# Edge weights in a PSUM bank of their own, and one bank for the state-space products

## The reference, cut to what matters

```python
proj = (x @ gat_w.T).reshape(n, NH, FOUT)                    # 4 heads of 64
e = leaky_relu(s_src[src] + s_tgt[tgt], 0.2)
exp_e = exp(e - max(e))
denom = segment_sum(exp_e, tgt)
agg = segment_sum(proj[src] * (exp_e / denom[tgt])[:, :, None], tgt)
...
xc, z = split(xs @ in_proj_w.T)          # xs = x[perm]
xc = silu(conv4(xc) + conv_b)
dbc = xc @ x_proj_w.T                    # 16 for dt, 16 for B, 16 for C
dt = softplus(dbc[:, :16] @ dt_proj_w.T + dt_proj_b)
h = exp(dt * A) * h + (dt * xc) * B      # scan over the nodes, 16 states per channel
y = (h @ C + xc * D_param) * silu(z)
out = y @ out_proj_w.T
```

## The kernel before, in words

| slot of TensorE | bank 0 | bank 1 |
|---|---|---|
| 2 | transpose of the input, `mb_x` (L1090) | output projection, `mb_y` (L1079) |
| 4 | turning of the output, `mb_o` (L1129) | input projection, first half (L1079) |
| 6 | input projection, second half (L1079) | |
| 9 | | projection to B, C, dt (L1106) |
| 11 | dt projection (L1113) | |

## Time and profile before

### The profile page before, as it was taken

One profiled execution on the slowest core, in us unless ns is written; L12 is line 12 of the kernel. 1 busy time (PEld: TensorE's weight loads), 2 busy tenths in 40 slices (PEclk: granted clock), 3 DMA queues, 4 the chain that ended last, 5 costly groups with the idle time before them and its releaser, 6 DMA issues. The chain is left out here.

```text
span 4467.2 us, 66228 instructions
## 1 busy us (share of the span) xinstructions
PE 3254.4 (73%) x18333; PEld 2554.5 (57%) x18334; DVE 3342.3 (75%) x6618; ACT 1430.2 (32%) x2818; POOL 2574.3 (58%) x2215
## 2 busy tenths in 40 slices
PE   5344220488878878888888888888888488848998
PEld 4333210366666666666666666666666345527887
DVE  5677793699988988899888898989888568831111
ACT  2000000244433344333443333443333256622222
POOL 2000004477777777777777777777777246643443
PEclk8555555599999999999999999999999699979999
DMA  3000201233333333333333333333335523326665
GB/s 109 20 0 0 96 1 59 75 97 97 97 96 98 99 96 96 95 95 98 97 96 96 96 97 98 96 97 96 93 99 91 109 58 98 85 84 151 143 143 110
DMA packets 217329, 397.02 MB, mean 89 GB/s; under 512 B 49239, under 2 KB 137544, under 8 KB 216776
## 3 DMA queue, kind: packets, MB, share of 16 engines
q0 software_dynamic: 119472, 287.74, 26.3%
q1 hardware_dynamic: 97560, 105.54, 7.7%
HBM read 330.21 MB, written 62.91 MB: 88 GB/s over the span
## 5 line engine op out<-in xcount | busy, mean ns | idle before, releaser
L664 POOL DMA_INDIRECT el_g<-table,el_ix x1792 | 2026.4, 1131 | 623.2 <-issue 455.3
L1050 PE MATMUL fl_ps<-el_g,el_oh 128*128 128x260 f32 x3584 | 935.3, 406 | 303.3 <-DVE ACC L773 300.3
L1050 PEld LDWEIGHTS fl_ps<-el_g,el_oh 128*128 128x128 f32 x3584 | 695.0, 200 | 662.1 <-issue 534.2
L929 ACT COPY el_oht<-fl_pt 128x512 f32<-128x512 f32 x452 | 262.7, 581 | 1217.3 <-PE fl_pt L1027 1217.3
L793 DVE TENSOR_TENSOR_SCAN mb_h<-mb_dA,mb_h,mb_dB 128x224 f32<-128x224 f32 x896 | 572.9, 669 | 85.3 <-issue 62.4
L763 DVE TENSOR_TENSOR el_g<-el_g 128x1024 f32<-128x1024 f32 x448 | 544.3, 1215 | 0.0
L1039 PEld LDWEIGHTS fl_px<-tile_score,el_oht 128*128 128x128 f32 x3608 | 484.1, 198 | 72.4 <-issue 53.5
L1039 PE MATMUL fl_px<-tile_score,el_oht 128*128 x3608 | 456.0, 256 | 28.3 <-issue 27.3
L1073 PE MATMUL fl_py<-mb_hc,ident 128*128 128x448 f32 x896 | 436.6, 570 | 0.1
L938 ACT ACTIVATE mb_dA<-mb_dt,mb_a 128x224 f32<-128x224 f32 x898 | 382.9, 476 | 106.4 <-DVE mb_dt L854 104.6
L1027 PE MATMUL fl_pt<-ident,el_oh 128*128 128x128 f32 x1808 | 302.4, 292 | 151.2 <-DVE el_oh L730 150.4
(11 more groups left out here) (290 smaller groups left out, 5161.4 us busy)
## 6 DMA issues: line engine op xcount, KB each, us to landing
el_g<-table,el_ix POOLq DMA_INDIRECT x1792, 2.8
ex_w<-in_moe_W SPq DMA_DIRECT2D x56, 512.0 KB
ex_x<-routed_x SPq DMA_DIRECT2D x56, 257.0 KB, 2.7
mb_x<-sorted_x SPq DMA_DIRECT2D x30, 224.0 KB, 2.8
table<-px_tr POOLq DMA_DIRECT2D x49, 130.0 KB, 2.4
px_x<-in_x SPq DMA_DIRECT2D x49, 128.0 KB, 2.8
xn<-XN SPq DMA_DIRECT2D x1, 6272.0 KB
sorted_y<-mb_or SPq DMA_DIRECT2D x28, 224.0 KB, 2.5
```

Of the source, the lines that this page charges most:

```text
L664: pool.indirect_dma_start(out=G[b // GU][:, b % GU * NJ + j, :], out_offset=None, in_=dram["table"], in_offset=bass.IndirectOffsetOnAxis(a ...
L1050: mm = nc.tensor.matmul(pS[:], OH[:, n % (2 * GU), j, :], G[n // GU % 2][:, n % GU * NJ + j, :], start=j == 0, stop=j == NJ - 1)
```

## The change

The weights get a PSUM bank of their own, `fl_pw`. ScalarE still writes the exponentials into `el_g` right after the logits, and writes them a second time into `fl_pw` at the end of its slot, after `give_out`, `prepare` and the decay; only the second write signals "weight". Since `fl_pw` holds one group of four slots, the second write waits until VectorE has scaled the last slot of the group before. The scaling reads the weights from `fl_pw` instead of from `el_g`.

To free that bank, all state-space products share one bank, `fl_pm`, so they follow each other: input transposed in TensorE's slot 0 (copied by ScalarE in slot 1), output projection in 2 (copied in 3), input projections in 4 and 6 (copied in 5 and 7), output turned in 8 (copied by ScalarE in slot 8 too), B, C and dt in 9 (10), dt projection in 11 (11). SyncE stores the output chunk after slot 10 instead of 6.

```diff
-        pY, pM = ps("fl_py", [P, KD, TC]), [ps(f"fl_pm{b}", [P, 512]) for b in range(2)]
+        pY, pM, pW = ps("fl_py", [P, KD, TC]), ps("fl_pm", [P, 512]), ps("fl_pw", [P, 512])
+        weight = pW[:, 0:GU * NJ * NH].rearrange("p (c h) -> p c h", h=NH)
...
-                nc.vector.tensor_tensor(rows, rows, G[g][:, at, D:].unsqueeze(3).to_broadcast([P, NJ, NH, FO]),
+                nc.vector.tensor_tensor(rows, rows, weight[:, at, :].unsqueeze(3).to_broadcast([P, NJ, NH, FO]),
...
             def prepare(c, b, at):          # ScalarE
-                if at == 3:
+                if at == 1:
                     act.wait_ge(s["xT"], c + 1)
-                    nc.scalar.copy(XT[:], wide(pM[0])).then_inc(s["xT_sb"], 1)
+                    nc.scalar.copy(XT[:], wide(pM)).then_inc(s["xT_sb"], 1)
...
             def give_out(c, at):            # ScalarE
-                elif at == 5:
+                elif at == 8:
                     act.wait_ge(s["oT"], c + 1)
...
-                    nc.scalar.copy(OR[:], pM[0][0:RB, :].rearrange("p (r d) -> p r d", r=TS)).then_inc(s["oT_sb"], 1)
+                    nc.scalar.copy(OR[:], pM[0:RB, :].rearrange("p (r d) -> p r d", r=TS)).then_inc(s["oT_sb"], 1)
...
             def slot(S):                    # ScalarE
-                    nc.scalar.activation(G[n // GU % 2][:, :, D:], DM[:], ACT.Exp).then_inc(s["weight"], 1)
+                    nc.scalar.activation(G[n // GU % 2][:, :, D:], DM[:], ACT.Exp)
                 if not early(c, 1):
                     give_out(c - 1, at)
                 prepare(c + 1, 1 - b, at)
                 decay(S + 1)
+                if n % GU == 0:
+                    if not early(S.number, 1):
+                        act.wait_ge(s["scaled"], S.number)
+                    nc.scalar.activation(weight, DM[:], ACT.Exp).then_inc(s["weight"], 1)
...
             def prepare(c, b, at):          # TensorE
-                if at == 2:
+                if at == 0:
                     pe.wait_ge(s["x"], (c + 1) * 16)
...
                 elif at == 6:
+                    pe.wait_ge(s["in_sb"], c + 1)
+                    project(pM, WI, XT, KD).then_inc(s["z_in"], 1)
+                elif at == 9:
+                    pe.wait_ge(s["z_sb"], c + 1)
                     if not early(c, 2):
                         pe.wait_ge(s["oT_sb"], c - 1)
...
             def give_out(c, at):            # TensorE
                 if at == 2:
                     pe.wait_ge(s["gated"], c + 1)
-                    pe.wait_ge(s["dt_row"], c + 2)
-                    pe.wait_ge(s["bx_rest"], c + 2)
-                    project(pM[1], WO, Y, 0).then_inc(s["o"], 1)
-                elif at == 4:
+                    pe.wait_ge(s["xT_sb"], c + 3)
+                    project(pM, WO, Y, 0).then_inc(s["o"], 1)
+                elif at == 8:
                     pe.wait_ge(s["o_sb"], c + 1)
-                    pe.wait_ge(s["xT_sb"], c + 3)
+                    pe.wait_ge(s["z_sb"], c + 3)
+                    turn_out()
```

More of the change, by code:

```diff
@@ L697, in slot @@
                     load(c + 2)
-                if at == 6 and not early(c, 1):
+                if at == 10 and not early(c, 1):
                     store(c - 1)
@@ L948, in prepare @@
                     act.wait_ge(s["in"], c + 1)
-                    nc.scalar.copy(XR[:, :, CONV - 1:], wide(pM[1])).then_inc(s["in_sb"], 1)
+                    nc.scalar.copy(XR[:, :, CONV - 1:], wide(pM)).then_inc(s["in_sb"], 1)
                 elif at == 7:
                     act.wait_ge(s["z_in"], c + 1)
-                    nc.scalar.activation(SZ[:, b], wide(pM[0]), ACT.Silu).then_inc(s["z_sb"], 1)
+                    nc.scalar.activation(SZ[:, b], wide(pM), ACT.Silu).then_inc(s["z_sb"], 1)
                 elif at == 8:
@@ L960, in prepare @@
                     act.wait_ge(s["bx"], c + 1)
-                    nc.scalar.copy(PARTS[0:2 * NS, b, :], pM[1][0:2 * NS, 0:TC]).then_inc(s["bx_hi"], 1)
+                    nc.scalar.copy(PARTS[0:2 * NS, b, :], pM[0:2 * NS, 0:TC]).then_inc(s["bx_hi"], 1)
                     act.wait_ge(s["bx_rest"], c + 1)
-                    nc.scalar.copy(DTR[2 * NS:, :], pM[1][2 * NS:BX, 0:TC]).then_inc(s["dt_row"], 1)
+                    nc.scalar.copy(DTR[2 * NS:, :], pM[2 * NS:BX, 0:TC]).then_inc(s["dt_row"], 1)
                     act.wait_ge(s["bx_mid"], c + 1)
@@ L984, in give_out @@
                     act.wait_ge(s["o"], c + 1)
-                    nc.scalar.copy(O[:], wide(pM[1])).then_inc(s["o_sb"], 1)
-                elif at == 5:
+                    nc.scalar.copy(O[:], wide(pM)).then_inc(s["o_sb"], 1)
+                elif at == 8:
                     act.wait_ge(s["oT"], c + 1)
@@ L1012, in _ @@
             give_out(NC - 1, 3)
[L1013 removed]
+            give_out(NC - 1, 8)
         @block.tensor
@@ L1110, in prepare, with turn_out @@
                     pe.wait_ge(s["dt_row"], c + 1)
-                    pe.wait_ge(s["z_sb"], c + 1)
+                    pe.wait_ge(s["bx_rest"], c + 1)
                     for m in range(KD):
-                        mm = nc.tensor.matmul(wide(pM[0])[:, m, :], WD[2 * NS:, m * P:(m + 1) * P], DTR[2 * NS:, :],
+                        mm = nc.tensor.matmul(wide(pM)[:, m, :], WD[2 * NS:, m * P:(m + 1) * P], DTR[2 * NS:, :],
                                               start=True, stop=True, skip_group_check=True)
                     mm.then_inc(s["dt_in"], 1)
+            def turn_out():
+                for r in range(TS):
+                    for k in range(KD):
+                        mm = nc.tensor.transpose(pM[0:RB, r * D + k * P:r * D + (k + 1) * P],
+                                                 O[:, k, r * RB:(r + 1) * RB], w["ident"][:])
+                mm.then_inc(s["oT"], 1)
             def give_out(c, at):
@@ L1119, in give_out @@
                     pe.wait_ge(s["gated"], c + 1)
-                    pe.wait_ge(s["dt_row"], c + 2)
-                    pe.wait_ge(s["bx_rest"], c + 2)
-                    project(pM[1], WO, Y, 0).then_inc(s["o"], 1)
-                elif at == 4:
+                    pe.wait_ge(s["xT_sb"], c + 3)
+                    project(pM, WO, Y, 0).then_inc(s["o"], 1)
+                elif at == 8:
                     pe.wait_ge(s["o_sb"], c + 1)
-                    pe.wait_ge(s["xT_sb"], c + 3)
-                    for r in range(TS):
-                        for k in range(KD):
-                            mm = nc.tensor.transpose(pM[0][0:RB, r * D + k * P:r * D + (k + 1) * P],
-                                                     O[:, k, r * RB:(r + 1) * RB], w["ident"][:])
-                    mm.then_inc(s["oT"], 1)
+                    pe.wait_ge(s["z_sb"], c + 3)
+                    turn_out()
             def slot(S):
@@ L1158, in _ @@
             pe.wait_ge(s["gated"], NC)
-            project(pM[1], WO, Y, 0).then_inc(s["o"], 1)
+            pe.wait_ge(s["v"], (NC + 1) * KD)
+            project(pM, WO, Y, 0).then_inc(s["o"], 1)
             pe.wait_ge(s["o_sb"], NC)
-            for r in range(TS):
-                for k in range(KD):
-                    mm = nc.tensor.transpose(pM[0][0:RB, r * D + k * P:r * D + (k + 1) * P],
-                                             O[:, k, r * RB:(r + 1) * RB], w["ident"][:])
-            mm.then_inc(s["oT"], 1)
+            turn_out()
 def nodes(nc, sem, w, a, dram):
```

14 lines of the change are left out of this document (5 added, 9 removed).

## The result

The changed kernel takes 4550.51 us (median of 4, 4549.45 to 4553.80), the kernel before 4478.07 beside it (4472.79 to 4479.94): a ratio of 1.0167, interval 1.0151 to 1.0183. The forecast was 4555.0. The profiled execution took 4550.16 and its span 4548.4, 81.2 us more than before, at the same mean granted clock of 0.868.

The account below looks back on a forecast made before the run. VectorE was busiest (75%), but ScalarE was taken as the bound in slots 8 and 9. 75.6 + 22 - 15 - 3, less 2 for gather waits, gave +78 on 4477: 4555 us, range 4530 to 4580.

Parts of the forecast that it names:

- The wait that the change puts in slot 8: ScalarE's copy in slot 8 waits for TensorE's turning; VectorE's wait before slot 9's scan grows 1.70 to 4.50: +75.6 us.
- Nothing swallowed: Later waits, the only candidate being slot 12's put down to gathers, absorb none of the 75.6 us.
- The rival that counted on 31 us: Partly swallowed: gather waits in slot 12 absorb 31 us, clock falls no more often; +27, 4504 us; chance 12%.
- rows 8 and 9: Slot 12's waits for gather or scores plus decay, in two chunks: 2.12 and 2.13 us together.
- The clock: TensorE's longer idle gap in slot 9 lowers its clock every chunk; 15 of 26 get new 1.5 us `mb_parts` waits: +22.
- The give-back in slot 4: Input transposes leave TensorE's slot 2 for slot 0, so slot 4's scores come 0.54 us earlier: 27 times, -15 us.
- The scaling: VectorE's scaling from PSUM gains at most 15 ns, 448 times; about half swallowed: -3 us, range -7 to +7.
- The rival of a much faster scaling: At L763 the PSUM operand shortens each scaling by 0.25 us, giving 4443 us; chance 4%.
- the estimate in the prediction: By the skill page's access overheads (about 60 ns SBUF, 125 ns PSUM), the scaling would cost 29 us more.
- At nothing: Costs counted as zero: second exponential behind the decay (32 us if uncovered), other moved copies, SyncE, everything outside the loop.
- GpSimd: By the skill's contention rule its gathers get shorter, but it is not awaited except in 43.9 us of waits.
- the dearer rival: TensorE comes back slow (+50 instead of +22) and PSUM reads cost 7: +118, 4595 us; chance 9%.

Follow-up runs that it names:

- The stall alone: Kernel before, two banks and weights in SBUF kept, only the output's turning and its copy moved to slot 8 (store to 10): 4807.59 us, 1.0302.
- second group: Follow-up kernels run on one chip where the kernel before took 4665.44 us; the changed kernel took 4874.85 us there, 1.0456.
- the stall undone: Changed kernel with ScalarE copying the turned output in slot 9 instead of 8: 4789.17 us (1.0244), repeated at 4788.60 us (1.0232).
- the shared bank alone: Changed kernel without the second exponential (weights read from SBUF) and with the turned output copied in slot 9: 4468.06 us, 0.9957.
- third group: Follow-up kernels run on a chip like that of the first comparison; the kernel before took 4490.51 us there.
- first group: Follow-up kernels run on one chip where the kernel before took 4669.68 us; the changed kernel itself was not among them.
- the decay first: Kernel before with ScalarE making the next slot's decay ahead of give_out and prepare: 4407.75 us, 0.9820.

## Why the prediction was right

The forecast was +78 us and the measured difference is +72.4 of the medians, +81.2 of the two profiled spans. The largest term and its mechanism are right; that the total fits so well is partly luck. The costs were forecast at 97.6 us (75.6 and 22) and come to 110 in VectorE's intervals over 26 chunks; the gains were forecast at 20 (15, 3 and 2) and come to 34, of which 22 lie in places for which the sum has no term (slots 0, 6 and 8). The two misses nearly cancel. Point by point:

- **The wait that the change puts in slot 8.** Right in place, cause and nearly in size: 4.42 instead of 1.70 in front of the scan of slot 9, where 4.50 was forecast. That is 27 x 2.72 = 73 us for the term of 75.6; in the last chunk alone it is 6.81. The stall alone brings a slowdown in the old kernel, undoing it gives 86 us in the second group, and without it and without the PSUM weights the kernel is at 0.9957. So the stall is shown to be the cause, and the shared bank is shown not to be. The stall was not undone by itself on a chip like that of the first comparison.
- **Nothing swallowed.** Right. Slot 12 kept its wait (2.11 per chunk before, 2.25 after). Of the 43.9 us "for gathers" the waits in slot 12, some 32 us, had been a label: they went away without a gain, and the wait for the decay grew by 23.4. The five in slot 8 were real but small, apart from one of 6.28 at the loop's end, which stays at 5.54. The rival that counted on 31 us fell on rows 8 and 9, as argued.
- **The clock.** The mechanism was right, the size too small: `mb_parts` is waited for in 27 places, not 11, with 1.69 each instead of 1.5, so +29 for the term of +22. The granted clock of 0.58 behind the gap and the vanishing of these waits when the gap was filled both show that it is the clock. Why filling it gained no time on its chip stays open.
- **The give-back in slot 4.** This term was mis-sized. It had -15; the wait for the scores went from 1.48 to 1.27, 27 x 0.21 = 6 us, and with the shorter waits around it the interval that ends in slot 4 went from 7.06 to 6.66, some 10 us in all. The term assumed that 0.54 taken from TensorE's queue in slot 2 reaches VectorE whole; 0.40 arrived, and no run shows where the rest stays. The prediction also says that no wait of VectorE's depends on what leaves slot 4 with the turning. That is wrong: the copy of the turned output left ScalarE's slot 5, and slot 6 got 0.28 shorter, 27 x 0.28 = 8 us. The gains in slots 0 and 8 (7 and 8 us) have no cause that a run shows.
- **The scaling.** 5 ns less, 448 times: -2 for -3. The rival of a much faster scaling is out, with 5 ns against the 170 that it needed.

  The Trainium skill, Perfetto Trace Analysis, Optimizing Scalar/DVE Operations, has a larger overhead for PSUM than for SBUF, by which the estimate in the prediction made the scaling 65 ns slower. The trace disagrees: 1210 ns against 1215. The scaling lost its second SBUF operand at the same time, and no run separates the two.
- **At nothing.** Right for the second exponential on the chip of the comparison: VectorE has no wait for `fl_pw`. "Outside the loop nothing changes" misses the 1.8 us of the first input projection. The two versions that issue it later show that the cover was real and thin (1.1 us per chunk as soon as it comes after the one-hot). On the chips of the first two groups it was perhaps not free: with the stall undone the changed kernel is still at 1.0232, where the shared bank alone is at 0.9957 on the third group's chip. No kernel with the weights in PSUM as its only change ran, and those two ratios are of different chips, so this cost is not shown, only likely.
- **GpSimd.** The trace agrees with the Trainium skill, SBUF — State Buffer, Who interferes with whom: the scaling has one SBUF input now and the gathers take 1007 ns instead of 1128. As forecast nobody waited for them, and the gain turned into GpSimd's idleness.

The forecast holds for a chip like that whose profile it was made from. On the second group's the changed kernel is 209 us slower than the one before, 1.8 times the dearer rival (+118).

## What to carry to other kernels

When buffers are merged, ask of every step that moves whether its producer still runs a slot ahead of its consumer; if both land in one slot, the consumer's wait delays all that stands behind it in its queue, and here that was the one thing VectorE needed next. An engine that is busy a third of the time can still set the pace: put what the busiest engine awaits first in its queue, and housekeeping with table loads behind it; that alone was worth 1.8% here, about as much as the change cost. A longer gap on TensorE was followed here by the lower clock, which put a second wait of 1.7 us per chunk on VectorE. When the terms of a sum miss in both directions, a good total doesn't show it: compare slot by slot.

## What the runs showed of the hardware that was not expected

- The same kernel took 4478 and 4491 us on two chips and 4670 and 4665 on two others. In its runs on the slower ones the mean granted clock was 0.84 to 0.85 instead of 0.86 to 0.87, and the profile has waits put down to "remote", of which the first comparison had none among VectorE's: 76.1 us in front of the logits in the changed kernel of the second group (1000 to 3580 us). The engine's own work did not slow down there (the scaling took 1210 ns there too). What holds TensorE up between its recorded instructions was not found; the stall of slot 8 is dearer there, 6.06 instead of 4.42.
- An exponential of 128x64 took 256 ns into the strided SBUF columns of `el_g` and 216 ns into PSUM.
- The gathers' issue on GpSimd got 11% shorter (1128 to 1007 ns) when another engine's instruction took one operand from PSUM. It was 998 to 1002 ns in three more runs with the weights in PSUM, and 1130 in the shared bank alone, where they are back in SBUF with the same bank. With the weights in SBUF it was 1115 on the first group's chip and 1096 with the decay first, so not all of the range is due to the operand.
- The gap of 2.16 us on TensorE in slot 9 was followed by the lower clock in 11 of 26 chunks, and the one of 4.6 us in all 27. The length of the gap is not all: in the shared bank alone 20 of 23 gaps of 2.3 to 2.4 us in front of the sums of slot 8 were followed by it, and with the decay first in the kernel before none of 8 gaps of 2.3 to 2.5 us at the same place.
